# Attention stage: the output bias is added by two rank-one products on TensorE instead of an addition to the rows of x on GpSimd

## The reference

```python
# x: (32, 128, 256); 16 heads of 16 features
n = layernorm(x)
Q = n @ wq.T + bq;  K = ctx @ wk.T + bk;  V = ctx @ wv.T + bv     # per head
s = where(mask == 0, 1e-9, Q @ K.T / 4)
x = x + (softmax(s) @ V) @ wo.T + bo
```

## Time and profile before

| | us |
|---|---|
| median of 3 runs | 1650.94 (1649.87 to 1651.84) |
| profiled execution | 1652.78, its span 1651.1 |
| mean granted TensorE clock | 0.872 of 2.4 GHz |

### The profile page before, as it was taken

One profiled execution on the slowest core, in us unless ns is written; L12 is line 12 of the kernel. 1 busy time (PEld: TensorE's weight loads), 2 busy tenths in 40 slices (PEclk: granted clock), 3 DMA queues, 4 the chain that ended last, 5 costly groups with the idle time before them and its releaser, 6 DMA issues. The chain is left out here.

```text
span 1651.1 us, 31760 instructions
## 1 busy us (share of the span) xinstructions
PE 1315.2 (80%) x10558; PEld 1072.3 (65%) x10559; DVE 1194.1 (72%) x2042; ACT 829.5 (50%) x1240; POOL 488.4 (30%) x483
## 2 busy tenths in 40 slices
PE   6189999999998629999268999999998499960087
PEld 3178888888897318998247777788887344320066
DVE  3979755566555569965278888888888677999854
ACT  4456433333332316633145555555555466887664
POOL 0236755555543033553121322222224000000000
PEclk9589999999999759999667888888888589985599
DMA  9567422322222656732510000000000100453211
GB/s 326 180 200 230 74 47 50 52 45 48 49 45 27 205 179 184 206 50 29 141 50 10 11 10 10 10 10 10 10 10 1 39 1 0 166 201 142 102 46 58
DMA packets 104262, 134.71 MB, mean 82 GB/s; under 512 B 16625, under 2 KB 88305, under 8 KB 102385
## 3 DMA queue, kind: packets, MB, share of 16 engines
q1 hardware_dynamic: 82672, 103.73, 19.0%
q0 software_dynamic: 21504, 29.83, 10.6%
HBM read 88.43 MB, written 45.11 MB: 81 GB/s over the span
## 5 line engine op out<-in xcount | busy, mean ns | idle before, releaser
L627 ACT ACTIVATE top_x_all<-top_h_ps,top_b1T 128x256 f32<-128x256 f32 x448 | 185.4, 474 | 308.2 <-PE top_h_ps L503 300.6
L501 PE MATMUL top_h_ps<-top_xT_hi,top_w_hi 128*128 128x256 f16 x896 | 245.7, 274 | 0.0
L502 PE MATMUL top_h_ps<-top_xT_lo,top_w_hi 128*128 128x256 f16 x896 | 245.6, 274 | 0.0
L503 PE MATMUL top_h_ps<-top_xT_hi,top_w_lo 128*128 128x256 f16 x896 | 245.6, 274 | 0.0
L519 PE MATMUL top_y_ps<-top_w_hi,top_x_all 128*128 x896 | 244.2, 273 | 0.0
L520 PE MATMUL top_y_ps<-top_w_lo,top_x_all 128*128 x896 | 244.2, 273 | 0.0
L521 PE MATMUL top_y_ps<-top_w_hi,top_x_all 128*128 x896 | 244.2, 273 | 0.0
L816 DVE CAST top_x_all<-top_x_all 128x512 f16<-128x512 f32 x224 | 98.1, 438 | 146.6 <-ACT top_x_all L627 146.6
L818 DVE TENSOR_TENSOR top_x_all<-top_x_all 128x512 f16<-128x512 f32 x224 | 155.6, 694 | 7.7
L355 POOL DMA_INDIRECT x_sum<-top_x_all,top_row_of_slot x56 | 94.5, 1688 | 175.3 <-DVE top_x_all L830 157.5
L1632 PE MATMUL ffn_ps<-ffn_dT_hi,ffn_yT 128*128 128x256 f16 x192 | 53.5, 278 | 107.2 <-DVE ffn_yT L1916 107.2
(11 more groups left out here) (297 smaller groups left out, 3195.7 us busy)
## 6 DMA issues: line engine op xcount, KB each, us to landing
top_staged<-in_L_xattn_W SPq DMA_DIRECT2D x32, 512.0 KB
top_staged<-in_L_ffn_w SPq DMA_DIRECT2D x32, 512.0 KB
up_raw<-ffn_u_all SPq DMA_DIRECT2D x48, 256.0 KB, 2.0
ffn_yT<-up_raw SPq DMA_DIRECT2D x12, 1024.0 KB, 4.8
top_w_lo<-in_ctx SPq DMA_DIRECT2D x4, 1024.0 KB, 9.6
top_x_all<-in_x SPq DMA_DIRECT2D x4, 1024.0 KB, 11.9
x_sum<-top_x_all SPq DMA_DIRECT2D x4, 1024.0 KB, 11.8
normed<-top_w_lo SPq DMA_DIRECT2D x4, 1024.0 KB, 4.6
```

What stands on the lines that cost most here:

```text
L501: nc.tensor.matmul(out, hi, xT_hi[p][:, c, :], start=(c == 0), stop=False)
L502: nc.tensor.matmul(out, hi, xT_lo[p][:, c, :], start=False, stop=False)
L503: last = nc.tensor.matmul(out, lo, xT_hi[p][:, c, :], start=False, stop=(c == DC - 1))
L627: last = nc.scalar.activation(h32[:, fc * R:(fc + 1) * R], h_ps[:, b, q * R:(q + 1) * R], ACT.Relu, bias=b1T[:, bass.ds(e * FC + fc, 1)], ...
```

## The change

The 32 additions on GpSimd and their semaphores go, and with them GpSimd's wait for the weights. VectorE prepares the bias once: `bo_hi` is 64 times bo in float16, `bo_lo` the rest, each one row of 256 on one partition. GpSimd fills a row of 128 ones. `out_product` gets two more matmuls, ones (1x128) by bo_hi and by bo_lo (1x256), which add 64 bo to all 128 rows of the PSUM tile; `finish` no longer waits for GpSimd.

```diff
+        ones = sb("ones", [1, P], F16)
+        bo_hi = sb("bo_hi", [1, D], F16)
+        bo_lo = sb("bo_lo", [1, D], F16)
...
             nc.gpsimd.memset(tiny[:], 1e-09).then_inc(s_const, 1)
+            nc.gpsimd.memset(ones[:], 1.0).then_inc(s_const, 1)
...
-            pool.wait_ge(s_w, 16 * 9)
...
-                this(pool, s_xn, m, p)
-                row = x_all[:, bass.ds(b, 1), :].rearrange("p a d -> p (a d)")
-                nc.gpsimd.tensor_tensor(row, row, biases[:, 3, :], ALU.add).then_inc(s_xb[p], 1)
...
-                    mm = nc.tensor.matmul(out, oT_lo[:, c, :], wT_hi[:, 3, c, :], start=False, stop=(c == DC - 1))
+                    nc.tensor.matmul(out, oT_lo[:, c, :], wT_hi[:, 3, c, :], start=False, stop=False)
+                nc.tensor.matmul(out, ones[:], bo_hi[:], start=False, stop=False)
+                mm = nc.tensor.matmul(out, ones[:], bo_lo[:], start=False, stop=True)
                 mm.then_inc(s_out[p], 1)
...
+            V.tensor_scalar(bo_hi[:], biases[0:1, 3, :], WEIGHT_SCALE, None, ALU.mult).then_inc(s_bo, 1)
+            dve.wait_ge(s_bo, 1)
+            order.tick(V.scalar_tensor_tensor(bo_lo[:], biases[0:1, 3, :], WEIGHT_SCALE, bo_hi[:], ALU.mult, ALU.subtract))
...
                 this(dve, s_out, m, p)
-                this(dve, s_xb, m, p)
```

More of the change, by code:

```diff
@@ L942, in attention @@
         s_pool = sem("pool_order"); s_dve = sem("dve_order"); s_const = sem("constants")
-        s_var = sem("variance"); s_root = sem("root"); s_prep = sem("dve_prepared")
+        s_var = sem("variance"); s_root = sem("root"); s_prep = sem("dve_prepared"); s_bo = sem("output_bias_high")
         s_wt = two("weights_transposed"); s_wh = two("weights_hi"); s_wl = two("weights_lo")
-        s_xn = two("xn_ready"); s_xb = two("x_biased")
+        s_xn = two("xn_ready")
         s_tp = two("inputs_transposed"); s_th = two("inT_hi_ready"); s_tl = two("inT_lo_ready")
@@ L1026, in _ @@
             nc.gpsimd.memset(tiny[:], 1e-09).then_inc(s_const, 1)
+            nc.gpsimd.memset(ones[:], 1.0).then_inc(s_const, 1)
             for i in range(4):
                 nc.gpsimd.memset(v32[i][:, :, DK:V1], 1.0).then_inc(s_const, 1)
-            pool.wait_ge(s_w, 16 * 9)
             def batch(m, p):
-                b = 2 * m + p
-                this(pool, s_xn, m, p)
-                row = x_all[:, bass.ds(b, 1), :].rearrange("p a d -> p (a d)")
-                nc.gpsimd.tensor_tensor(row, row, biases[:, 3, :], ALU.add).then_inc(s_xb[p], 1)
                 this(pool, s_qh, m, p)
@@ L1059, in _ @@
         def _(pe):
-            pe.wait_ge(s_const, 7)
+            pe.wait_ge(s_const, 8)
             pe.wait_ge(s_w, 16 * 9)
@@ L1285, in _ @@
             scales(slice(0, QB), 1)
-            dve.wait_ge(s_const, 7)
+            dve.wait_ge(s_const, 8)
             def between(n):
```

## The result

| | before | after |
|---|---|---|
| median | 1651.39 (1649.87 to 1653.03, 4 runs) | 1673.85 (1672.72 to 1677.78, 4 runs) |
| profiled execution, its span | 1652.78, 1651.1 | 1674.15, 1672.5 |
| mean granted TensorE clock | 0.872 | 0.863 |

The ratio is 1.014, with a 95% interval of 1.0121 to 1.0159: the changed kernel is slower by 1.4%. Of the profiled execution's 21.4 us, nearly all lies in the attention stage.

A forecast was written before the change was run, and what follows sets the result against it. No engine is full; a 13.64 us chain across engines bounds each attention slot. Steady slots 9.5, head 1.4, tail 2.8 and preparation 0.55 make 14.2 us, giving 1665; range 1652.5 to 1676.

The forecast's parts named there:

- likeliest case: Attention stage: the plain sum, each steady slot 0.38 us longer, 14.2 us in all, 1660 to 1668; chance 0.40.
- rival 2: Steady slots: TensorE's clock stays down in some, each costing 3.5 + 0.7 us; total 1669 to 1682, chance 0.21.
- Removed work: GpSimd's 32 additions of 1.7 us and finish's wait for them: removing them is worth nothing.
- contention: VectorE's second masked copy, 2.06 us, seems to wait for GpSimd's L1042, not the removed addition, so should stay near 2.06.
- Price of the added work: TensorE's output product: two one-row matmuls and two tile changes take 0.71 us at 1.2 GHz, 0.38 at 2.4.
- change of tile: Switch between 128-row and one-row matmuls on TensorE: two per output product, together 0.28 us at 1.2 GHz or 0.17 at 2.4.
- w: Time the added products put on each slot at the fast clock; the prediction took 0.38 us.
- Rival 1: Steady slots: the clock gives most back, slots return to 13.65 us; +3.8 us, 1654.7; chance 0.23.
- lag: How far the clock falls ahead of TensorE's resumption after the exponentials; forecast 0.74 us, between harmless 0.42 and long-stretch 0.82.
- Preparation, head and tail: Outside steady slots: VectorE's bias preparation 0.55 us, two head slots 1.4, five tail slots 2.8.
- Rival 3: Steady slots: busier TensorE keeps the clock up in some, each saving 1.79 us; thirteen give 1642; chance 0.06.
- the ring: Attention slot's chain of dependent steps over several engines, output product included; one turn takes 13.64 us.

The follow-up runs named there:

- full-height version: Changed kernel with two 128-row products, identity weights by the bias on all partitions, in place of the one-row ones; ratio 1.0027 to the kernel before.
- two versions that add 0.22 and 0.30: Changed kernel with two 128-row products for the one-row ones (1.0027), and changed kernel without ones by bo_lo (1.0033), both against the kernel before.
- version with four full-height products: Changed kernel with the bias added by two 128-row identity products plus two more with zero moving operands; ratio 1.0091 to the kernel before.

## Why the prediction was right, and where it was not

The measured 1673.85 lies in the range, on the side that was forecast, 9 us above the point. This is partly luck: it lies outside the 1660 to 1668 of the likeliest case, and the range holds it because it took in the lower two thirds of rival 2 (1668 to 1682), which had a chance of 0.21. The forecast was 14 us more, measured were 22.

*Removed work: right.* The addition and its wait were worth nothing (1.0004 without them), and the contention is with L1042, as the earlier trace rows were read.

*Price of the added work: right.* Forecast were 0.71 us at 1.2 GHz and 0.38 at 2.4. In the slot shown, the stretch grew by 0.46, with the first change of tile (0.14) at 1.2 GHz and both products (0.12, then 0.11) and the second change (0.09) at 2.4. The one-row products were neither free nor dearer than their columns, and did not all lie in the slow stretch, as the prediction had it. The slots say the same: with the clock falling 0.22 to 0.64 ahead, a slot should take 13.64 less half of that and plus w; 13.91, 13.82 and 13.74 give w = 0.38, 0.42 and 0.42.

*The case that was taken for the likeliest: wrong.* The sum let every slot be longer by 0.38 and arrived at 14.02. No slot of the steady part took that; their mean, 14.34, is reached only through the long ones. The step that failed is the one from the price to the sum: it counted the price once for each slot, though the earlier trace rows already showed that the falls of the clock do not move with the slots. The full-height version shows what such a step misses: 0.22 a slot would be 5.3 us in 24 slots, and its slots are 13.66.

*The rivals that came true: 1 and 2, one after the other.* Rival 1 describes each slot of the cycle but the long one and the one behind it, and all steady slots of the two versions that add 0.22 and 0.30. Rival 2 describes the rest. It gave a long slot as 17.2 + 0.7 = 17.9, measured 17.80; a quick one that returns 1.4 against 13.65, measured 12.41 or 1.24; one more slow stretch, 3.4 us, for each cycle, measured 17.2 in five; a lag between 0.42 and 0.82 as the limit, measured between 0.68 and 0.70; and 18 to 31 us in all, measured 22.5 by the medians. It had the right mechanism with a chance of 0.21. What would have raised it was in the text: a lag that settles at 0.74, next to one observation at 0.82 where the clock stayed down, with nothing between 0.42 and 0.82 to say that 0.74 was safe.

*Preparation, head and tail.* Preparation and head were put at 2.0 and came to -0.9: the changed kernel lost the long slow stretch of the slot of 876.16. The tail was put at 2.8 and took 4.7. The sum counted 0.38 for its first slot, which gained a fall and 1.8 us. In both places the sum counted added work where the place of the falls decided.

*Rival 3* was possible after all, but not by this change. Its 0.4 us sits behind the resumption; put ahead of it, the same 0.43 us still left every steady fall in place, and so did 0.7 us of other matmuls. 0.9 us took them all away.

## What to carry to other kernels

A repeating loop like this one can have a slow stretch of TensorE that repeats on a beat of its own, here 13.65 us. Then time added to the ring or taken from it is not time of the kernel: small additions vanish, and a slightly larger one tips single turns into 4 us more. Before costing an edit, look where in the turn the granted clock falls and how the distance changes from turn to turn, and try to fill the wait ahead of it first, with different amounts: seven matmuls brought nothing to the steady part and nine brought it all. Work given to TensorE belongs where it waits anyway, not behind the wait: the same two matmuls cost 22 us in one place and 3 in the other.

## What the runs showed that I had not expected

- In the steady part of the kernel before, the slow stretch costs 13.64 - 12.18 = 1.46 us in every slot, 36.5 us in 25 slots, and nine matmuls that nobody reads remove it; seven leave every steady slot as it was (ratio 0.9963, its small gain not traced).
- In the steady part a lag of up to 0.68 us was harmless and one of 0.70 cost a slot of 17.8 us (15.25 in the version with four full-height products, at 0.74).
- One-row and 64-row products of 256 columns cost the same: 1.0142 and 1.014 of the kernel before.
